# Attention row maxima turned on VectorE in 32-blocks, strided query tiles, and eight row transfers from two queues

## The reference, cut to what matters

```python
x = x + attention(layernorm(x))      # 16 heads of 16, with biases
x = x + ffn(layernorm(x))            # silu(x W1) * (x W3), Hadamard transform, W2
x = x + memory(layernorm(x))         # gates and a decaying scan over the sequence
x = x + ffn(layernorm(x))
```

```python
scores = jnp.einsum('bhqd,bhkd->bhqk', Q, K) / jnp.sqrt(jnp.float32(Hd))
attn = jax.nn.softmax(scores, axis=-1)
out = jnp.einsum('bhqk,bhkd->bhqd', attn, V)
```

## Time and profile before

| | |
|---|---|
| median of 3 runs | 586.35 us (586.34 to 586.47) |
| the profiled execution | 586.26 us |
| its span (first to last instruction) | 584.4 us |
| attention loop, K = 0 to 127 | 44.8 to about 251 us of the span |
| granted TensorE clock | 0.999 of full speed |
| PE busy / DVE busy / ACT busy / POOL busy | 565.8 / 376.8 / 298.5 / 176.6 us |

### The profile page before, as it was taken

How to read it: one execution, slowest core, us unless ns; L and a number is a source line. 1 busy time by engine, 2 the same in 40 slices (tenths; PEclk the granted TensorE clock), 3 DMA queues, 4 the chain that set the end, 5 groups by cost and what they waited for, 6 DMA issues and landing times.

```text
span 584.4 us, 8867 instructions
## 1 busy us (share of the span) xinstructions
PE 565.8 (97%) x3288; PEld 390.1 (67%) x3288; DVE 376.8 (64%) x718; ACT 298.5 (51%) x546; POOL 176.6 (30%) x193
## 2 busy tenths in 40 slices
PE   9899999999999988999999999999999999999997
PEld 4534334344334433368888888898777888888886
DVE  5498898898888899644363444558887436344433
ACT  3238878876886787752334242244445233424221
POOL 3956446354455242820101010014333010101000
PEclk9999999999999999999999999999999999999999
DMA  7654740240033030010000000000000010010101
GB/s 231 135 112 163 199 122 18 76 127 20 2 111 109 3 146 3 3 72 2 1 0 1 1 0 1 2 2 0 1 0 2 1 36 1 1 36 2 38 0 37
DMA packets 17891, 26.54 MB, mean 45 GB/s; under 512 B 2552, under 2 KB 10744, under 8 KB 17464
## 3 DMA queue, kind: packets, MB, share of 16 engines
q1 hardware_dynamic: 15992, 24.13, 13.6%
q10 hardware_dynamic: 1856, 1.84, 1.4%
HBM read 10.88 MB, written 5.24 MB: 28 GB/s over the span
## 4 chain that ended last, share of the span: by engine, by line
PE 85%; DVE 5%; ACT 4%; issue 2%; DMA 1%; POOL 1%; SPq 1%; DVEq 0%; ACTq 0%
PE PS L281 82%; PE PS L292 2%; DVE mxr L861 2%; ACT PR L735 1%; DMA ring<-ql 1%; DVE PR L1020 1%; ACT xf L644 1%; ACT qf L658 1%; DVE XNs L842 1%; ACT PR L788 1%; POOL xTl L1051 1%; ACT xTh L644 1%; PE PS L472 1%; DVE AOl L853 1%; SPq L214 1%
## 5 line engine op out<-in xcount | busy, mean ns | idle before, releaser
L281 PE MATMUL PS<-xTh,ring 128*128 128x512 f32 x608 | 188.5, 392 | 0.0
L861 DVE TENSOR_REDUCE mxr<-PS 128x1 f32<-128x512 f32 x256 | 163.0, 682 | 29.0 <-PE PS L281 28.7
L735 ACT ACTIVATE PR<-PS 128x512 f32<-128x512 f32 x256 | 137.8, 603 | 39.7 <-PE PS L281 39.7
L281 PEld LDWEIGHTS PS<-xTh,ring 128*128 128x128 f32 x608 | 113.2, 188 | 22.9 <-issue 0.8
L281 PE MATMUL PS<-xTl,ring 128*128 128x512 f32 x304 | 110.3, 391 | 0.4 <-POOL xTl L1051 0.4
L281 PE MATMUL PS<-ring 50*128 50x512 f32 (+1 forms) x512 | 98.2, 450 | 5.4 <-DVE mxr L861 4.9
L975 DVE TENSOR_TENSOR PR<-PR,PS 128x512 f32<-128x512 f32 x64 | 43.8, 684 | 91.6 <-PE PS L281 73.7
L281 PEld LDWEIGHTS PS<-ring 50*128 50x128 f32 (+1 forms) x512 | 41.2, 184 | 84.2 <-ACT PR L735 57.2
L644 ACT ACTIVATE AOh<-PR 128x512 fp32r<-128x512 f32 x72 | 45.5, 632 | 101.1 <-DVE PR L975 89.2
L1051 POOL TENSOR_TENSOR xTl<-xf,xTh 128x512 fp32r<-128x512 f32 x30 | 43.2, 1456 | 140.9 <-ACT xTh L644 140.9
L853 DVE TENSOR_TENSOR AOl<-PR,AOh 128x512 fp32r<-128x512 f32 x72 | 51.1, 710 | 50.3 <-ACT AOh L644 50.3
(11 more groups left out here) (98 smaller groups left out, 621.5 us busy)
## 6 DMA issues: line engine op xcount, KB each, us to landing
ring<-qh SPq DMA_DIRECT2D x52, 128.0 KB, 3.1
ring<-ql SPq DMA_DIRECT2D x26, 128.0 KB, 3.1
ring<-weight_scratch SPq DMA_DIRECT2D x3, 1024.0 KB, 4.9
weight_scratch<-in_w SPq DMA_DIRECT2D x2, 1024.0 KB, 6.8
out<-X SPq DMA_DIRECT2D x8, 256.0 KB, 2.2
X<-in_x SPq DMA_DIRECT2D x3, 512.0 KB, 5.2
PR<-in_w SPq DMA_DIRECT2D x1, 1024.0 KB, 7.6
ring<-AOh SPq DMA_DIRECT2D x8, 128.0 KB, 4.0
```

The costliest lines, as they stand in the source:

```text
L281: return nc.tensor.matmul(dst, lhsT, rhs, start=start, stop=stop, skip_group_check=True)
L735: nc.scalar.activation(PR[:, j % 8, :], PS[:, kq_bank(j), :], ACT.Exp, scale=HD ** -0.5)\
L861: nc.vector.tensor_reduce(mxr[:, S % 2, blk, TT * p + t:TT * p + t + 1], PS[:, QK0 + i % 3, :], AX.X, ALU.max, negate=True).then_inc(max_d ...
```

## The change

Three things change together.

1. The tile `ms` becomes 128 x 4 x 32 (one block of 32 columns for each query tile t; 24 of the 32 columns stay zero, set once by POOL). VectorE turns it in blocks of 32 x 32 (`turn_max`), once per group, at the end of step s % 8 == 3 behind that step's two row maxima. The transpose on TensorE (16 of them), the copy on ScalarE (16) and their waits go. The waits that order the use of bank MB are rewritten to name the evacuation before them.
2. Product `score_qk` number t takes each fourth query (`t:SEQ:TT`) as its stationary operand where it took 128 neighbours. With that the turned block holds 128 neighbouring queries on each partition used.
3. A turned row is spread over four partitions, so each of the 8 rows that a group needs (2 halves, high and low, 2 pairs) is one transfer of 4 rows of 128. SP issues the four of half 0, POOL issues the four of half 1 directly behind its `split_max`. SP's place in its loop is s % 8 == 4 (was 5), between the same ring loads as before.

```diff
-MAX_AT = 5
+MAX_AT = 4
...
-        ms = sb("ms", [P, 2, 2, 2 * TT])
-        mT = sb("mT", [32, P])
+        ms = sb("ms", [P, TT, 32])
+        mT = sb("mT", [P, P])
...
+        def max_row_copies(S, blk):
+
+            b, g = S // GROUPS, S % GROUPS
+            return [(ring[HALF * blk + MROW + k:HALF * blk + MROW + k + 1, b % 2, QI, 2 * g + p, :].bitcast(F32),
+                     mT[16 * p + 2 * blk + k:P:32, :]) for k in range(2) for p in range(2)]
...
             def max_rows(S):
...
-                for blk in range(2):
-                    r = HALF * blk + MROW
-                    sp.dma_start(ring[r:r + 2, b % 2, QI, 2 * g:2 * g + 2, :].bitcast(F32),
-                                 mT[16 * blk:16 * blk + 16, :]).then_inc(mrow_in, DMA)
+                for to, src in max_row_copies(S, 0):
+                    sp.dma_start(to, src).then_inc(mrow_in, DMA)
...
-                mm(PS[:, QK0 + i % 3, :], ring[r:r + KROWS, b % 2, QI, p, t * P:(t + 1) * P],
+                mm(PS[:, QK0 + i % 3, :], ring[r:r + KROWS, b % 2, QI, p, t:SEQ:TT],
                    ring[r:r + KROWS, b % 2, KI, p, :], True, True).then_inc(s1_ready, 1)
...
-                    pe.wait_ge(mrow_in, 2 * DMA * (K // 8 + 1))
+                    pe.wait_ge(mrow_in, 4 * DMA * (K // 8 + 1))
+                    pe.wait_ge(mrow_in2, 4 * DMA * (K // 8 + 1))
...
-                        nc.tensor.transpose(MB[0:32, 0:P], ms[:, :, :, :].rearrange("p a b k -> p (a b k)"),
-                                            ident[:, :]).then_inc(mps_ready, 1)
...
-            def max_evacuate(S):
-                act.wait_ge(mps_ready, S + 1)
-                if S:
-                    act.wait_ge(mrow_in, 2 * DMA * S)
-                hi(mT[:, :], MB[0:32, 0:P]).then_inc(mt_ready, 1)
...
+            def turn_max(S):
+
+                dve.wait_ge(ml_done, S + 1)
+                if S:
+                    dve.wait_ge(mrow_in, 4 * DMA * S)
+                    dve.wait_ge(mrow_in2, 4 * DMA * S)
+                nc.vector.transpose(mT[:, :].rearrange("p (i t) -> p t i", t=TT), ms[:, :, :]).then_inc(mt_ready, 1)
...
+                    if U == 8 and h == 0:
+                        turn_max(0)
...
+                if s % 8 == 3 and (K + 5) // 8 < LAST_GROUP:
+                    turn_max((K + 5) // 8)
...
-                m = mxr[:, S % 2, :, :]
-                nc.gpsimd.tensor_copy(ms[:, :, 0, :].bitcast(F32R), m).then_inc(mh_done, 1)
+                m = mxr[:, S % 2, :, :].rearrange("q b (p t) -> q b p t", p=2)
+                high, low = (ms[:, :, :].rearrange("q t (p y b k) -> q k b p t y", p=2, y=4, b=2)[:, k, :, :, :, 0]
+                             for k in range(2))
+                nc.gpsimd.tensor_copy(high.bitcast(F32R), m).then_inc(mh_done, 1)
                 pool.wait_ge(mh_done, S + 1)
-                nc.gpsimd.tensor_tensor(ms[:, :, 1, :].bitcast(F32R), m, ms[:, :, 0, :], ALU.subtract).then_inc(ml_done, 1)
+                nc.gpsimd.tensor_tensor(low.bitcast(F32R), m, high, ALU.subtract).then_inc(ml_done, 1)
+
+            def max_rows(S):
+
+                pool.wait_ge(mt_ready, S + 1)
+                for to, src in max_row_copies(S, 1):
+                    pool.dma_start(to, src).then_inc(mrow_in2, DMA)
...
                 if s % 8 == 3 and (K + 5) // 8 < LAST_GROUP:
                     split_max((K + 5) // 8)
+                    max_rows((K + 5) // 8)
```

More of the change, by code:

```diff
@@ L143, in build @@
         ring_in = [sem(f"ring_in{n}") for n in range(4)]
-        s1_ready, max_done, mh_done, ml_done, mps_ready, mt_ready, mrow_in = (
-            sem(n) for n in ("s1_ready", "max_done", "mh_done", "ml_done", "mps_ready", "mt_ready", "mrow_in"))
+        s1_ready, max_done, mh_done, ml_done, mt_ready, mrow_in = (
+            sem(n) for n in ("s1_ready", "max_done", "mh_done", "ml_done", "mt_ready", "mrow_in"))
         st_ready, exp_done, av_done, ot_done, rec_done, otn_done, aof_ready, aoh_done, aol_done, wo_ready, x_done = (
@@ L156, in build @@
                              "load_done", "lh_done", "ll_done"))
-        out_done = sem("out_done")
+        out_done, ms_zero, mrow_in2 = (sem(n) for n in ("out_done", "ms_zero", "mrow_in2"))
         def rows(qk, n_part, blk):
@@ L432, in _ @@
                     pe.wait_ge(xns_ready, 1)
-                    pe.wait_ge(mt_ready, 1)
                     ln_transpose(0, MB)
@@ L437, in _ @@
                     keep_busy(1, PS[:, 2, :], FILL)
[L438 to L441, removed]
             pe.wait_ge(w2h_done, FT // 2)
             def shared_bank(K, b, s):
-                more, turned = b < BATCH - 1, K + LEAD
+                more = b < BATCH - 1
                 if s == LN_AT[0] and more:
                     pe.wait_ge(xns_ready, b + 2)
-                    pe.wait_ge(mt_ready, turned // 8)
+                    pe.wait_ge(v_copied, 2 * (b + 2))
                     ln_transpose(0, MB)
@@ L478, in shared_bank @@
                                 pe.wait_ge(x_f, 2 * (b + 1))
-                            elif n == 2:
-                                pe.wait_ge(qk_f, 4 * b + 2)
                             else:
-                                pe.wait_ge(mt_ready, turned // 8)
+                                pe.wait_ge(qk_f, 4 * b + n)
                         i = 3 * QK_AT[n].index(s)
@@ L489, in shared_bank @@
                     else:
-                        pe.wait_ge(mt_ready, turned // 8)
+                        pe.wait_ge(x_f, 2 * (b + 1))
                     for part in range(2):
@@ L493, in shared_bank @@
                 if s in OUT_AT[1] and b:
-                    if s == OUT_AT[1][0]:
-                        pe.wait_ge(mt_ready, turned // 8)
+                    if s == OUT_AT[1][0] and more:
+                        pe.wait_ge(v_copied, 2 * (b + 1) + 1)
+                    elif s == OUT_AT[1][0]:
+                        pe.wait_ge(x_done, 2 * b - 1)
                     out_projection(1, OUT_AT[1].index(s))
@@ L507, in shared_bank @@
                     elif s == V_AT[1][0]:
-                        pe.wait_ge(mt_ready, turned // 8)
+                        pe.wait_ge(v_copied, 3)
                     project_v(b + 1, 1, V_AT[1].index(s))
@@ L716, in _ @@
             for j in range(FT // 2):
-                if j == FT // 2 - 1:
-                    max_evacuate(0)
                 act.wait_ge(had_ready, j + 1)
@@ L741, in _ @@
                     ln_evacuate(b + 1, 1, MB)
-                if s % 8 == MAX_AT and (K + LEAD) // 8 - 1 < LAST_GROUP:
-                    max_evacuate((K + LEAD) // 8 - 1)
                 if b < BATCH - 1:
@@ L1104, in _ @@
             nc.gpsimd.memset(eps[:, :], EPS).then_inc(pool_init, 1)
+            nc.gpsimd.memset(ms[:, :, :], 0.0).then_inc(ms_zero, 1)
             nc.gpsimd.memset(Vp[:, :, :, HD:HD + 1], 1.0).then_inc(pool_init, 1)
@@ L1131, in _ @@
             split_max(0)
+            max_rows(0)
             pool.wait_ge(whi_done, 4)
```

5 lines of the change are left out of this document (3 added, 2 removed).

## The result

The changed kernel takes 602.55 us (median of 4 runs, 599.97 to 605.11) against 586.35 before: a ratio of 1.028 with a 95% interval of 1.0232 to 1.0328, that is 13.6 to 19.2 us more. The forecast was +7.1. The sign and the range held; the size is wrong, and the largest loss was not in it.

The account below looks back on a forecast made before the run. Attention was taken as bound by TensorE, except two stretches (about 73 to 87 and 206 to 231 us) bound by VectorE. Terms -4.7 + 2.1 + 9.7 = +7.1 us on 586.26 gave 593.4 us, range 583.0 to 607.

Parts of the forecast that it names:

- Term 4: Strided weight loads of the score products on TensorE: taken as zero, with 25 us kept for the range.
- Rival B: Strided weight loads of score products are exposed: slower, 603 to 612 us with the prediction's sum; chance 0.12.
- What bounds the kernel: In attention TensorE sets the pace, except about 73 to 87 and 206 to 231 us, where VectorE does.
- Term 1: TensorE's transposes of the maxima go: 0.47 us at six and 0.38 at five of 15, 4.7 us gained.
- Term 2: VectorE's turn, 0.28 us each plus its wait for POOL's low part: 2.1 us lost where VectorE leads.
- Term 3: The eight row transfers per group, four on POOL: rows arrive late and TensorE waits, 9.7 us lost.
- c: Price of one transfer issued by POOL: taken as 0.96 us, the middle of bounds 0.63 and 1.28.
- POOL's backlog: Bias addition, low parts and layer norm tiles queued behind POOL's wait and 3.8 us of transfers per group: costed at nothing.
- A: Nothing arrives late, POOL's transfers cost what SP's do: faster, 583.8 us; chance 0.29.
- C: POOL falls behind, a transfer at 1.28 us, waits for rows summing to some 30 us: 613 us; chance 0.06.
- D: The turn makes VectorE the bound everywhere: some 5 us, slower; chance 0.02.

Follow-up runs that it names:

- s1: Kernel before, with each score taking every fourth query, so the subtracted maximum is another query's: 599.14 us against 586.01, ratio 1.0226.
- s2: Changed kernel with 128 neighbouring queries per score again, the subtracted maximum being another query's: 591.85 us, ratio 1.0088.
- s3: Changed kernel with POOL's layer norm tiles of batch 2 one step earlier (steps 23 to 26 of batch 0): 599.48 us, ratio 1.0228.
- s4: Changed kernel with both edits, layer norm tiles one step earlier and contiguous queries per score: 589.02 us, ratio 1.0048.
- e5: Changed kernel, but for groups 4 and 15 SyncE sends all eight rows and GpSimd none: 598.89 us, ratio 1.0214.
- e6: Changed kernel with SyncE sending all eight rows for groups 4 and 15, and contiguous queries per score: 588.95 us, ratio 1.004.
- e9: Kernel before without TensorE's 15 turns at the MAX_AT steps, pieces of the identity sent instead, waits and ScalarE's copies kept: 584.24 us, ratio 0.9967.
- e11: Kernel before with 15 more 128x128 turns of the identity by VectorE into a spare buffer, waiting for nothing: 586.32 us, ratio 1.0002.
- e10: Kernel before with every second query of a half (8 bytes apart) as a score's stationary operand: 586.11 us, ratio 1.0001.
- e8: Changed kernel with 12 transposes of the identity where TensorE waits for XNs at batch 0 step 30: 600.38 us against 602.55.

## Why the prediction went wrong

**Term 4, zero: measured +13.1 alone (s1), 10 to 10.7 in the change** (changed kernel less s2 10.7, s3 less s4 10.5, e5 less e6 9.9). This is the step that failed. The argument was that all loads of 128 columns in the rows have one price whatever they read; but all of them read contiguously, so the rows could not tell. Its own upper bound, a load of 0.11 us more with all of it exposed in each pair, gave 25. Measured is a load of 0.12 us more, of which 0.055 per pair shows. Rival B, given 0.12, was the mechanism.

**What bounds the kernel.** This reading holds: in the changed kernel too VectorE holds TensorE up in the steps where it did before, by 3.5 us of waits for maxima. Nothing in it speaks of the loads, which lengthen TensorE's steps where it leads.

**Term 1, -4.7 us: about right, and e9 does not contradict it.** The 1.65 us of e9 is not the price of a turn with its waits, since the waits stayed. The reading from starts came out where it could be seen: 0.47 us at the step of the earlier trace rows in e6. In the changed kernel against s1, which has the same strided queries and TensorE's turns, the 15 steps gain between 0.36 us and nothing (in one, step 5 of batch 3, the loss of term 2 is larger). The gains add up to 2.8 us, an estimate from the starts of value products in two profiles. The 4.7 was somewhat too high.

**Term 2, +2.1 us: about 0.9 in the changed kernel, by the mechanism that was forecast.** A turn takes 408 ns, not 340, and it waits for POOL's low part as read from the earlier trace rows: 6.3 us in 8 waits, longest 1.0, against a forecast of 1.1. Where VectorE leads, this passes on to TensorE: behind step 19 of batch 0 the changed kernel loses 0.57 us against s1, and behind step 3 of batch 3 0.29. The sum of TensorE's waits for maxima does not show it (4.8 us, 4.9 before). With contiguous queries it is 6.2: 0.4 us at step 13 of batches 0 to 2 is new, where the prediction had the late turn absorbed. By e11 the turn's own work costs nothing, so what costs is, as far as these runs show, its wait.

**Term 3, +9.7 us: measured at least +3.7, by another mechanism.** The term was mis-sized at c: 0.58 us a transfer for an assumed 0.96, and a landing of 1.6 for 1.92. Taking the middle between bounds by the likeness to a routine of POOL had nothing behind it; SP's 0.63 was the row of the same kind of operation. TensorE does not wait for rows in the profile of the changed kernel. In s2, s3, s4, e5 and e6 it waits 0.6 to 1.6 us for those of group 2, where the landing took long. What also failed is the sentence that costed POOL's backlog at nothing. It named the queue but neither the layer norm tile's due step nor group 15's neighbours. 3.7 us is the changed kernel less e5 (3.1 of it already by s3), the wait and the clock behind it together; e5 has 0.8 us of late rows in exchange, and the transfers of the other 14 groups stay in it, so what those cost was not measured. The backlog was to show as a late `divide`; it showed as a late `XNs` and as one long cast. The Trainium skill (DMA: Bandwidth & Descriptors, Latency and other measured facts) gives about 1 us to the first byte of a transfer from GpSimd; no row here shows a first byte, and 1.0 us put in for c, as the prediction did beside its sum, would have been further off.

**The sum.** The stride alone is +13.1 us (s1), and the changed kernel is 3.4 us above s1: together 16.5, with 16.2 seen. Without the stride the other terms make 5.8 us (s2), against a forecast of 7.1; the two parts hide some of each other. That the first three terms come near as a sum is luck: 9.7 us of waits for rows, most of which never came, stood in for a late layer norm tile, a fall of the clock and a long cast. The sign of the forecast was right for the same reason, and the strided loads, most of the loss, were not in it.

**The rivals.** A's mechanism (nothing late, transfers at SP's price) held in the profile of the changed kernel and did not help. C had POOL falling behind with rows late by 30 us; POOL fell behind, with no rows late there. D did not occur: fifteen turns added nothing (e11).

No version that computes the right result beats the kernel before. e9 does not bound what the removal of TensorE's turns can bring, because its waits stayed. A layout in which the 32-blocks' rows leave so that a score takes every second query, which e10 shows to be free, would by my count need more transfers than eight a group, and wasn't tried.

## What to carry to other kernels

Where a change gives an operand a stride that no row has, the price of that operand is unknown, however many rows of its size agree; test the one access pattern alone first. When an experiment takes an instruction away, look where its waits went: if they stay in the program, the run prices something else than the change. When a queue is blocked for some us, look up the due time of each thing queued behind it at every repetition, not only the typical one: here two of 16 groups made TensorE wait for what stood behind the transfers, and moving those two gave 3.7 us back. And before comparing two kernels in the same window of time, check that the same steps run in it.

## What was not expected of the hardware

- A stationary operand's load, 128 float32 columns: about 192 ns at a distance of 8 bytes, 250 at 12 and 307 at 16, where contiguous ones take 184.
- An idle stretch of 2.2 us on TensorE was followed by 8 us at a granted clock of 0.50, and one of 1.93 us in s4 by about 6; with products of the identity in place of the first (e8) the clock stayed at 1.00. The fall cost 4 to 5 us, about twice the wait. It did not come each time: behind 1.83 us at the attention's end the changed kernel's clock stayed at 1.00, behind 1.84 at the same place in s3 it fell.
- A cast of 128x512 on VectorE took 0.38 us alone and 1.5 in turn with POOL's passes over tiles of the same size. Where POOL's four passes came directly behind its transfers, one cast took 6.27 us and ended 0.3 us behind the fourth pass.
- A transfer of 2 KB issued by POOL kept it for 0.56 us in the median (0.80 at most); SP's four of group 4 took 2.22 us, 0.56 each. POOL's mostly landed 1.6 us after their issue. To its engine POOL's queue was hardly dearer than SP's.
